# Soft experts on one Trainium2 core: the residual enters by VectorE and is turned back by the products that transpose the result

## The chip, the core and the metric

The kernel runs on one core of a Trainium2 chip. Five engines work side by side: TensorE (PE, with its weight loads listed as PEld), VectorE (DVE), ScalarE (ACT), GpSimd (POOL) and SyncE (SP, which here only issues DMAs). They are ordered by semaphores alone. The metric is the time of one execution in microseconds on the device. Lower is better.

## The reference

A small language-model tower: byte features, a neighbourhood attention, a mixture of experts of which two are used for each token, a decayed attention, and last a layer of soft experts. Every layer but the first adds its result to its input `h` after a layer norm. The last layer is the one that the change is about:

```python
def _L1_ffn_ref(x, Wr, br, W1, b1, g1, be1, m1, v1, W2, b2, g2, be2, m2, v2, Wo, bo):
    feat = jnp.mean(x, axis=0)
    w = jax.nn.softmax(feat @ Wr + br, axis=-1)
    h = jax.nn.relu(_bn(jnp.einsum('bfd,edh->bfeh', x, W1) + b1, g1, be1, m1, v1))
    h = jax.nn.relu(_bn(jnp.einsum('bfeh,ehk->bfek', h, W2) + b2, g2, be2, m2, v2))
    y = jnp.einsum('bfeh,ehd->bfed', h, Wo) + bo
    return jnp.einsum('bfed,fe->bfd', y, w)
...
h = h + _L1_ffn_ref(_layernorm(h, axis=-1), ...)
```

There are 32 batches (b) of 512 tokens (f) with 64 channels (d), and 8 experts (e), all in float32.

## The kernel before

**Layout.** Two batches make a pair; a pair is a tile of 128 partitions (64 channels of each batch) by 512 tokens. The residual stream `s.h` holds all 16 pairs in SBUF, and so does the normed input `s.z`, whose rows from 16 on are scratch (rows 16 to 19 hold the routing weights `f1_w` and row 20 the shift `f1_r` in the last layer).

**The turned basis.** Between the first layer and the last, `h` is kept multiplied by a 64x64 reflection (`house`, block-diagonal for the pair; `reflect` is its vector), which puts the mean of the channels into channel 0, so that the layer norm has no subtraction. A reflection is its own inverse. So the weights that write into `h` are turned once at the start: `turn_rows` (L600) takes blocks of 64 columns of `s.w_out` in four VectorE instructions (product with the vector L606, sum L609, outer product L612, subtraction L615). It runs inside `token_features`: steps 0 and 1 in the loop's round q = 5, step 2 in q = 6, step 3 in q = 7 (L860 to L867). TensorE waits for step 3 (L767) before the product L768 that turns the weights which read `h`; behind L768 on TensorE stand the last pair's tokens (L743), whose squares (GpSimd, L494) feed the last variance (L501), the norm's deviations (ACT, L798, L800) and then, by two DMAs, the first input of the next stage. Of the 18 blocks in `s.w_out` the first 9 are turned (`W_TURNED`); the last layer's output weights `f1_wo` and `raw_bo` are not among them.

**The last layer, `soft_experts` (L1816).** 64 steps, four for a pair, each for two experts (`ep`). A step has on TensorE `first` (4 products into `p_1`, L1853), `second` (4 into `p_2`, L1863) and `third` (2 into `p_y`, L1874, which sums over the pair's four steps); on ACT a ReLU between first and second (L1899, two instructions); on VectorE `weigh` between second and third (L1921: clamp and routing weight). TensorE issues them staggered and in this order in each round n: first of step n+3, second of n+2, third of n+1, turn of n. `second` waits for the ReLU of its own step and for `weigh` of the step before, as there is one `p_2`.

Once for each pair three more things happen. Ahead of the pair's first `third`, TensorE multiplies `house` with the pair's `h` into `p_y` (L1872), which brings the residual back to the plain basis. After its last `third`, VectorE adds the shift: `res = p_y + f1_r` (L1931), and TensorE turns `res` into rows of tokens by four 128x128 transposes with the identity (L1885, the stationary operand is every fourth column of `res`). ACT copies them (L1908) and SP writes them out (L1948). `third` of a new pair waits for `res` of the pair before. GpSimd does nothing in this stage.

**The stage ahead, `soft_router` (L1720),** computes the routing weights and the shift. Its L1765 is a full float32 product of 128x128 by 128x128, 16 times. The stages are separated by a barrier of all engines.

In the records each float32 product is two matmul instructions with a weight load each, and each float32 transpose is one.

Of the kernel before, what the change touches and what calls it, by code (L numbers as in the profile page):

```python
# [25 lines left out]
ALU = mybir.AluOpType  # L26
# [3 lines left out]
NB, T, D = 32, 512, 64  # L30
NP = NB // 2
NQ = NB // 4
# [3 lines left out]
EP = NE // 2  # L36
NH, DH = 8, 8
HL = NH // 2
ROUTES = 32
W_OUT, W_TURNED = 18, 9  # L40
KW, DIL = 31, 2
TG = T // DIL
QT = 32
# [82 lines left out]
def allocate(nc, ctx):  # L126
    s = Buffers()

    def sb(name, shape, dt=F32):
        return ctx.enter_context(nc.sbuf_tensor(name, shape, dt))  # L130

    s.const = sb("const", [128, CONST_COLS])
    s.h = sb("h", [128, NP, T])
    s.z = sb("z", [128, NB, T])
    s.pick = sb("pick_r", [128, EP, 128], F32R)
    s.winmask = sb("winmask_b", [128, 4, HL, WIN], BF16)
    s.ident_b = sb("ident_b", [128, 128], BF16)

    s.w1s = sb("tok_w1s", [128, HID])
    s.phase = sb("tok_phase", [128, 2, NQ])  # L140
    s.gram = sb("tok_gram", [128, 128])
    s.cross = sb("tok_cross", [128, NQ])
    s.bias_t = sb("tok_bias_t", [128, HID])
    s.tok_w2 = sb("tok_w2", [128, D])

    s.w_in = sb("w_in", [128, T])
    s.a0_wqk = s.w_in[:, 0:256].rearrange("p (c n) -> p c n", c=2)
    s.a0_wv, s.moe_wr, s.f1_wr, s.a1_wqk = s.w_in[:, 256:384], s.w_in[:, 384:416], s.w_in[:, 416:448], s.w_in[:, 448:512]
    s.moe_w1 = sb("moe_w1", [128, NE, D])
    s.f1_w1 = sb("f1_w1", [128, NE, D])  # L150
    s.w_out = sb("w_out", [128, W_OUT, D])
    s.a0_wp, s.moe_w2, s.f1_wo, s.raw_bo, s.raw_moe_b2, s.a1_wvk = [s.w_out[:, n:n + m, :] for n, m in ((0, 2), (2, EP), (10, EP), (14, EP), (6, 2), (8, 2))]
    s.moe_b2 = sb("moe_b2", [128, 128], F32R)
    s.a1_bvk = sb("a1_bvk", [128, 2, D])
    s.f1_br = sb("f1_br", [128, NE])
    s.f1_w2 = sb("f1_w2", [128, NE, D])
    s.f1_wdup = sb("f1_wdup", [128, EP, 2, D])
    s.f1_w = s.z[:, NP:NP + EP, :]
    s.f1_r = s.z[:, NP + EP, :]
    s.bn_diag = sb("bn_diag", [128, EP, 128])  # L160

    s.raw = sb("raw", [128, 3 * (NE + EP)])
    at = 0

    def part(*shape):
        nonlocal at
        n = int(np.prod(shape))
        at += n
        return s.raw[:, at - n:at]

    s.bn_var, s.bn_scale, s.bn_shift = part(NE + EP), part(NE + EP), part(NE + EP)
    s.loaded = ctx.enter_context(nc.semaphore("loaded"))
    s.bn_ready = ctx.enter_context(nc.semaphore("bn_ready"))
    s.sq, s.bc = [[sb(f"n_{x}{k}", [128, T]) for k in range(n)] for x, n in (("sq", 8), ("bc", 4))]
    s.rstd = sb("n_rstd", [128, NP // 4, T])
    s.n_sq, s.n_var, s.n_ln, s.n_rstd, s.n_z, s.n_zero, *s.n_hop = [ctx.enter_context(nc.semaphore("n_s_" + x)) for x in (
        "sq", "var", "ln", "rstd", "z", "zero", "hop0", "hop1", "hop2", "hop3")]
    s.n_bc = [ctx.enter_context(nc.semaphore(f"n_s_bc{k}")) for k in range(4)]
    s.spread = nc.dram_tensor("n_spread", (4, NP // 4, 128, T), F32).ap()
    s.eps = sb("eps", [128, 1])  # L180
    s.one = sb("one", [128, 1])

    s.cols = sb("cols", [128, COL_COUNT])
    return s
# [13 lines left out]
def const(s, name, rows=128):  # L198
    at, n = CONST_AT[name]
    return s.const[0:rows, at:at + n]  # L200
# [334 lines left out]
def done(n):  # L535

    return n + (1 + CREDITS)
# [7 lines left out]
def row(t, n):  # L545

    return t[:, bass.ds(n, 1), :].rearrange("p a b -> p (a b)")
# [70 lines left out]
def token_features(nc, s, a, windows):  # L618


    with ExitStack() as ctx:
# [12 lines left out]
        g = [s.z[:, 4 + 2 * n:6 + 2 * n, :] for n in range(4)]  # L634
        bias_rows = s.z[:, 12:14, :].rearrange("p a (q h) -> p (a q) h", h=HID)
        rstd = s.z[:, 14, :]
        tmp = s.z[:, NP + NQ:NP + NQ + 2, :].rearrange("p a (n d) -> p (a n) d", d=D)[:, 0:W_TURNED, :]
        split, own = sb("split", [64, T], 1, F32R)[0], sb("own", [64, NB, NF], 1, F32R)[0]
        squared, offset = sb("squared", [128, HID], 1)[0], sb("offset", [128, 1], 1)[0]
        total = sb("total", [128, W_TURNED + 2], 1)[0]  # L640
# [4 lines left out]
        block = ctx.enter_context(nc.Block())  # L645
# [1170 lines left out]
def soft_experts(nc, s, out):  # L1816


    with ExitStack() as ctx:
# [3 lines left out]
        def ps(name, shape, n=1):  # L1823
# [3 lines left out]
        a1, a2 = sb("a1", [128, 2, T]), sb("a2", [128, 2, T])  # L1827
        res, rows = sb("res", [128, T]), sb("rows", [128, 2, 4, D])
        p_1, p_2, p_y, p_t = ps("p1", [128, 2, T], 2), ps("p2", [128, 2, T])[0], ps("py", [128, T])[0], ps("pt", [128, T])[0]
        s_w1, s_a1, s_w2, s_a2, s_wo, s_res, s_t, s_rows, *s_zin = [  # L1830
            ctx.enter_context(nc.semaphore("se_" + x)) for x in ("w1", "s_a1", "w2", "s_a2", "wo", "s_res", "t", "s_rows", "zin0", "zin1")]
        s_out = [ctx.enter_context(nc.semaphore(f"se_out{k}")) for k in range(2)]
        block = ctx.enter_context(nc.Block())

# [2 lines left out]
            return at.k // EP, at.k % EP  # L1837

        half = [slice(0, 64), slice(64, 128)]

        @block.tensor
        def _(te):
            give_credits(te, s_w1, s_w2, s_wo, s_t)

            def first(at):
                slot, ep = where(at)
                if ep == 0:
                    te.wait_ge(s_zin[slot], at.of(8) * 32 + 32)
                te.wait_ge(s_a1, done(at.n - 2))
                for e2 in range(2):  # L1850
                    for b in range(2):
                        z = row(s.z, at.of(4)) if b == e2 else swapped[slot]
                        mm = nc.tensor.matmul(p_1[at.k % 2][half[b], e2, :], s.f1_w1[half[e2], 2 * ep + e2, :], z[half[e2], :],  # L1853
                                              start=True, stop=True, skip_group_check=True)
                mm.then_inc(s_w1, 1)

            def second(at):
                _, ep = where(at)
                te.wait_ge(s_a1, done(at.n))
                te.wait_ge(s_a2, done(at.n - 1))  # L1860
                for b in range(2):
                    for e2 in range(2):
                        mm = nc.tensor.matmul(p_2[half[e2], b, :], s.f1_w2[half[b], 2 * ep + e2, :], a1[at.k % 2][half[b], e2, :],  # L1863
                                              start=True, stop=True, skip_group_check=True)
                mm.then_inc(s_w2, 1)

            def third(at):
                _, ep = where(at)
                te.wait_ge(s_a2, done(at.n))
                if ep == 0:  # L1870
                    te.wait_ge(s_res, done(at.of(4) - 1))
                    nc.tensor.matmul(p_y[:], const(s, "house"), row(s.h, at.of(4)), start=True, stop=False, skip_group_check=True)  # L1872
                for b in range(2):
                    mm = nc.tensor.matmul(p_y[half[b], :], s.f1_wo[:, ep, :], a2[at.k % 2][:, b, :], start=False, stop=(ep == EP - 1),  # L1874
                                          skip_group_check=True)
                mm.then_inc(s_wo, 1)

            def turn(at):
                slot, ep = where(at)
                if ep == EP - 1:  # L1880
                    i = at.of(4)
                    te.wait_ge(s_res, done(i))
                    te.wait_ge(s_rows, done(i - 1))
                    for c in range(4):
                        mm = nc.tensor.transpose(p_t[:, c * 128:c * 128 + 128], res[slot][:, c::4], const(s, "ident"))  # L1885
                    mm.then_inc(s_t, 1)

            unrolled(EP * NP, 8, (3, first), (2, second), (1, third), (0, turn))
# [24 lines left out]
        @block.vector  # L1913
        def _(ve):
            give_credits(ve, s_a2, s_res)

            def weigh(at):
                _, ep = where(at)
                ve.wait_ge(s_w2, done(at.n))
                ve.wait_ge(s_wo, done(at.n - 2))  # L1920
                nc.vector.scalar_tensor_tensor(out=a2[at.k % 2][:], in0=p_2[:], scalar=col(s, "f1_be2", ep),  # L1921
                                               in1=s.f1_w[:, ep, :].unsqueeze(1).broadcast_to([128, 2, T]),
                                               op0=ALU.max, op1=ALU.mult).then_inc(s_a2, 1)

            def residual(at):
                slot, ep = where(at)
                if ep == EP - 1:
                    i = at.of(4)
                    ve.wait_ge(s_wo, done(at.n))
                    ve.wait_ge(s_t, done(i - 2))  # L1930
                    nc.vector.tensor_tensor(res[slot][:], p_y[:], s.f1_r, ALU.add).then_inc(s_res, 1)  # L1931

            unrolled(EP * NP, 8, (1, weigh), (0, residual))

# [56 lines left out]
```

## Time and profile before

| | |
|---|---|
| median of 3 runs | 989.21 us (987.61 to 993.39) |
| the profiled execution | 995.81 us, its span 993.8 us |
| granted TensorE clock, mean over the span | 0.932 of full speed |
| busy: PE, DVE, ACT, POOL | 87%, 53%, 47%, 27% |
| `soft_experts` | from 769 us to the end |

The span runs from the first to the last instruction of one execution; 2.0 us lie around it. Busy shares are means over the whole span. In the timeline rows below, a row is a run of instructions of one kind on one engine: its start, its length, and in brackets the engine's idle time before it with what ended that. Matmuls are pipelined: the length of one is longer than the distance from its start to the next one's start, so costs are taken from the distances.

### The profile page before, as it was taken

What the parts mean: (1) busy time and instruction counts of PE and PEld (TensorE: products, weight loads), DVE (VectorE), ACT (ScalarE), POOL (GpSimd) and SP (SyncE); (2) the same over time, 40 slices, a digit from 0 to 9 for tenths busy, and PEclk for the clock granted to TensorE, in tenths of its full rate; (3) what the DMA queues carried; (4) which work ended last, traced back from release to release, by engine and by line L of the source; (5) the groups of instructions that cost most, each with busy time, mean ns of one, the idle gap of its engine ahead of it and who ended that gap; (6) DMA issues with size and microseconds to landing.
All of it is one profiled execution on the core that took longest, in us unless ns stands there. A gap on an engine that the chain in (4) does not pass through costs nothing. (4 is left out here: it accounts for less than half of the span.)

```text
span 993.8 us, 28180 instructions
## 1 busy us (share of the span) xinstructions
PE 865.4 (87%) x12432; PEld 412.2 (41%) x12432; DVE 527.3 (53%) x719; ACT 469.4 (47%) x579; POOL 268.3 (27%) x270
## 2 busy tenths in 40 slices
PE   4796899989899994699999792988876899999997
PEld 2231577767667672122222120766644222222222
DVE  5443567757667673676675251656631344344443
ACT  3243477767777763344444442233321454444543
POOL 4044553524435233122211046324541000000000
PEclk9898899999999998799999796889977899999999
DMA  4201200010010011000000113223221111111110
GB/s 87 32 11 63 78 25 25 5 56 4 4 57 4 17 44 54 1 1 1 1 1 1 63 53 112 49 58 90 69 66 40 32 43 43 44 43 43 36 30 33
DMA packets 39771, 37.76 MB, mean 38 GB/s; under 512 B 21025, under 2 KB 25282, under 8 KB 39650
## 3 DMA queue, kind: packets, MB, share of 16 engines
q1 hardware_dynamic: 38578, 34.35, 12.6%
q8 instruction: 99, 1.62, 0.7%
q10 hardware_dynamic: 1072, 1.60, 0.5%
q14 instruction: 22, 0.18, 0.1%
HBM read 19.95 MB, written 7.60 MB: 28 GB/s over the span
## 5 line engine op out<-in xcount | busy, mean ns | idle before, releaser
L1921 DVE SCALAR_TENSOR_TENSOR se_a<-se_p,cols,z 128x1024 f32<-128x1024 f32 x64 | 82.1, 1284 | 137.9 <-PE se_p L1863 137.9
L1899 ACT ACTIVATE se_a<-se_p,cols 128x512 f32<-128x512 f32 x128 | 92.6, 773 | 81.9 <-PE se_p L1853 81.9
L1189 DVE TENSOR_REDUCE na_rowmax<-na_ps 128x16 f32<-128x1024 f32 x64 | 78.0, 1218 | 77.6 <-PE na_ps L1065 77.6
L1481 DVE TENSOR_TENSOR me_gw<-me_pc,me_g 128x1024 f32<-128x1024 f32 x64 | 78.3, 1223 | 76.3 <-PE me_pc L1336 71.7
L1377 ACT ACTIVATE me_g<-me_p,cols 128x1024 f32<-128x1024 f32 x64 | 71.3, 1114 | 86.7 <-PE me_p L1324 82.0
L923 POOL TENSOR_TENSOR z<-na_k,const 128x512 f32<-128x512 f32 x64 | 64.5, 1039 | 141.2 <-ACT na_k L1129 141.2
L494 POOL TENSOR_TENSOR n_sq<-h 128x512 f32<-128x512 f32 x64 | 67.4, 1058 | 110.8 <-DVE h L846 43.8
L529 POOL TENSOR_TENSOR z<-h,n_bc 128x512 f32<-128x512 f32 x62 | 78.5, 1283 | 25.5 <-DMA n_bc<-n_spread 25.5
L1324 PE MATMUL me_p<-z,moe_w 64*64 64x512 f32 x512 | 74.0, 650 | 6.4 <-ACT me_g L1377 6.4
L1192 DVE TENSOR_TENSOR na_e<-na_ps,na_rowmax 128x1024 f32<-128x1024 f32 x64 | 78.3, 1224 | 2.2
L1853 PE MATMUL se_p<-z,f_w 64*64 64x512 f32 x256 | 71.2, 628 | 4.0 <-DMA se_zswap<-z 4.0
L1074 PE MATMUL na_pt<-const,na_e 128*128 128x128 f32 x512 | 69.2, 278 | 2.5 <-ACT na_et L1159 1.7
L1346 PE MATMUL me_py<-me_gw,w_out 128*64 128x512 f32 x256 | 70.8, 632 | 0.4 <-DVE me_gw L1481 0.4
L1853 PE MATMUL se_p<-se_zswap,f_w 64*64 64x512 f32 x256 | 70.3, 628 | 0.0
L1874 PE MATMUL se_py<-se_a,w_out 128*64 128x512 f32 x256 | 69.0, 618 | 0.4 <-DVE se_a L1921 0.4
L1159 ACT ACTIVATE na_et<-na_pt 128x1024 f32<-128x1024 f32 x64 | 65.4, 1022 | 7.8 <-PE na_pt L1074 7.0
L1863 PE MATMUL se_p<-se_a,f_w 64*64 64x512 f32 x512 | 67.4, 597 | 1.1 <-DVE se_a L1921 1.1
L1152 ACT ACTIVATE na_e<-na_e 128x1024 f32<-128x1024 f32 x64 | 67.4, 1053 | 1.7 <-DVE na_e L1192 1.3
L1263 POOL TENSOR_TENSOR h<-h,me_added 128x512 f32<-128x512 f32 x16 | 20.6, 1290 | 155.3 <-DVE me_added L1489 155.3
L1074 PEld LDWEIGHTS na_pt<-const,na_e 128*128 128x128 f32 x512 | 56.0, 140 | 13.9 <-issue 11.2
L1146 ACT ACTIVATE na_v<-na_pm 64x512 f32<-64x512 f32 x64 | 38.6, 602 | 33.7 <-PE na_pm L1025 33.3
L1091 PE MATMUL na_po<-na_v,na_et 128*32 128x18 f32 x4096 | 49.4, 187 | 4.1 <-issue 2.7
(282 smaller groups left out, 1274.9 us busy)
## 6 DMA issues: line engine op xcount, KB each, us to landing
n_bc<-n_spread SPq DMA_DIRECT2D x128, 128.0 KB, 3.0
da_zswap<-z SPq DMA_DIRECT2D x32, 128.0 KB, 2.4
se_zswap<-z SPq DMA_DIRECT2D x32, 128.0 KB, 2.3
out<-se_rows SPq DMA_DIRECT2D x16, 256.0 KB, 2.1
n_spread<-n_rstd SPq DMA_DIRECT2D x13, 256.0 KB, 2.0
const<-in_const ACTq DMA_DIRECT2D x1, 712.0 KB, 6.5
const<-in_const ACTq DMA_DIRECT2D x1, 562.0 KB, 4.2
f_w<-in_L_ffn_W SPq DMA_DIRECT2D x4, 128.0 KB
```

The source lines that it names most:

```text
L529: return eng.tensor_tensor(row(s.z, p), row(s.h, p), s.bc[p % 4][:], ALU.mult)
L1074: mm = nc.tensor.transpose(p_t[:, c, :], e[b][:, 2 * c:2 * c + 2, :].rearrange("p h w -> p (h w)"), const(s, "ident"))
L1189: nc.vector.tensor_reduce(rowmax[b][:], scored, AX, ALU.max).then_inc(s_max, 1)
L1192: nc.vector.tensor_tensor(e[b][:], scored, rowmax[b][:].unsqueeze(2).broadcast_to([128, GROUPS, WIN]), ALU.subtract).then_inc(s_diff, 1)
L1324: mm = nc.tensor.matmul(p_1[half[e2], b, :], s.moe_w1[half[b], 2 * ep + e2, :], row(s.z, at.of(4))[half[b], :], start=True, stop=True, ski ...
L1346: mm = nc.tensor.matmul(p_y[slot][half[b], :], s.moe_w2[:, ep, :], gw[at.k % 2][:, b, :], start=False, stop=(ep == EP - 1), skip_group_che ...
L1377: nc.scalar.activation(g[at.k % 2][:], p_1[:], ACT.Gelu, bias=col(s, "moe_b1", ep)).then_inc(s_g, 1)
L1481: nc.vector.tensor_tensor(gw[at.k % 2][:], p_c[:], g[at.k % 2][:], ALU.mult).then_inc(s_gw, 1)
L1853: mm = nc.tensor.matmul(p_1[at.k % 2][half[b], e2, :], s.f1_w1[half[e2], 2 * ep + e2, :], z[half[e2], :], start=True, stop=True, skip_grou ...
L1874: mm = nc.tensor.matmul(p_y[half[b], :], s.f1_wo[:, ep, :], a2[at.k % 2][:, b, :], start=False, stop=(ep == EP - 1), skip_group_check=True)
L1899: ins = nc.scalar.activation(a1[at.k % 2][:, e2, :], p_1[at.k % 2][:, e2, :], ACT.Relu, scale=col(s, "f1_g1", 2 * ep + e2), bias=col(s, "f ...
L1921: nc.vector.scalar_tensor_tensor(out=a2[at.k % 2][:], in0=p_2[:], scalar=col(s, "f1_be2", ep), in1=s.f1_w[:, ep, :].unsqueeze(1).broadcast ...
```

## The change

In `soft_experts` the product of `house` with `h` is taken out. The first `third` of a pair starts the sum in `p_y` itself. GpSimd adds the shift to `h` of all 16 pairs at the start of the stage; VectorE adds `h` (now with the shift in it) instead of the shift. The result is then still in the turned basis, and the four transposes become four float32 products with `house` in place of the identity, which transpose and turn back at once. So that `f1_wo` and `raw_bo` write into the turned basis, the blocks of `s.w_out` are put in another order, and the first 17 of 18 are turned.

```diff
-W_OUT, W_TURNED = 18, 9
+W_OUT, W_TURNED = 18, 17
...
-    s.a0_wp, s.moe_w2, s.f1_wo, s.raw_bo, s.raw_moe_b2, s.a1_wvk = [s.w_out[:, n:n + m, :] for n, m in ((0, 2), (2, EP), (10, EP), (14, EP), (6, 2), (8, 2))]
+    s.f1_wo, s.raw_bo, s.a0_wp, s.moe_w2, s.raw_moe_b2, s.a1_wvk = [s.w_out[:, n:n + m, :] for n, m in ((0, EP), (4, EP), (8, 2), (10, EP), (14, 2), (16, 2))]
...
-        tmp = s.z[:, NP + NQ:NP + NQ + 2, :].rearrange("p a (n d) -> p (a n) d", d=D)[:, 0:W_TURNED, :]
+        tmp = s.z[:, NP + NQ:NP + NQ + 3, :].rearrange("p a (n d) -> p (a n) d", d=D)[:, 0:W_TURNED, :]
...
+        @block.gpsimd
+        def _(pool):
+            for p in range(NP):
+                nc.gpsimd.tensor_tensor(row(s.h, p), row(s.h, p), s.f1_r, ALU.add).then_inc(s_shifted, 1)
...
                 if ep == 0:
                     te.wait_ge(s_res, done(at.of(4) - 1))
-                    nc.tensor.matmul(p_y[:], const(s, "house"), row(s.h, at.of(4)), start=True, stop=False, skip_group_check=True)
                 for b in range(2):
-                    mm = nc.tensor.matmul(p_y[half[b], :], s.f1_wo[:, ep, :], a2[at.k % 2][:, b, :], start=False, stop=(ep == EP - 1),
+                    mm = nc.tensor.matmul(p_y[half[b], :], s.f1_wo[:, ep, :], a2[at.k % 2][:, b, :], start=(ep == 0), stop=(ep == EP - 1),
                                           skip_group_check=True)
...
-                        mm = nc.tensor.transpose(p_t[:, c * 128:c * 128 + 128], res[slot][:, c::4], const(s, "ident"))
+                        mm = nc.tensor.matmul(p_t[:, c * 128:c * 128 + 128], res[slot][:, c::4], const(s, "house"), start=True, stop=True, skip_group_check=True)
...
                     ve.wait_ge(s_wo, done(at.n))
+                    ve.wait_ge(s_shifted, i + 1)
                     ve.wait_ge(s_t, done(i - 2))
-                    nc.vector.tensor_tensor(res[slot][:], p_y[:], s.f1_r, ALU.add).then_inc(s_res, 1)
+                    nc.vector.tensor_tensor(res[slot][:], p_y[:], row(s.h, i), ALU.add).then_inc(s_res, 1)
```

## Rows read from the trace of the kernel before

**Rows 1.** The page: span, and the granted TensorE clock in 40 slices.
```profile
span 993.8 us, 28180 instructions
...
PEclk9898899999999998799999796889977899999999
```

**Rows 2.** The page: the chain that ended last, by line, share of the span.
```profile
PE se_p L1853 7%; PE se_py L1874 6%; PE se_p L1863 6%; PE se_py L1872 2%; PE se_pt L1885 1%; DVE se_a L1921 0%; DMA se_zswap<-z 0%; DVE se_res L1931 0%; ACT se_rows L1908 0%; SPq L1944 0%; PEldq L542 0%
```

**Rows 3.** Busy time by stretch: PE, PEld, DVE, ACT, POOL, clock, DMA, GB/s.
```profile
768.00:784.00 16.00, 11.34 (x63) 2.75 (x62) 2.57 (x2) 5.65 (x9) 0.00 (x0) 0.79 0.14 33
784.00:988.00 204.00, 203.12 (x1314) 57.48 (x1310) 88.53 (x77) 96.46 (x137) 0.00 (x0) 1.00 0.14 38
```

**Rows 4.** Timeline, one pair of `soft_experts`, from its `house` product to the next.
```profile
859.07 1.12 PE L1872 MATMUL se_py<-h,const 128*128 128x512 f32 x2
...
860.13 1.08 PE L1874 MATMUL se_py<-se_a,w_out 128*64 128x512 f32 x4
...
861.14 0.75 PE L1885 MATMUL se_pt<-const,se_res 128*128 128x128 f32 x4
...
861.82 0.64 PE L1853 MATMUL se_p<-z,f_w 64*64 64x512 f32 x1
...
869.61 1.28 DVE L1921 SCALAR_TENSOR_TENSOR se_a<-se_p,cols,z 128x1024 f32<-128x1024 f32 x1 [1.60 <-PE se_p L1863]
...
870.81 0.68 DVE L1931 TENSOR_TENSOR se_res<-se_py,z 128x512 f32<-128x512 f32 x1
...
871.39 1.04 PE L1863 MATMUL se_p<-se_a,f_w 64*64 64x512 f32 x8
...
872.35 1.12 PE L1872 MATMUL se_py<-h,const 128*128 128x512 f32 x2
```

**Rows 5.** Timeline, `soft_router`: full products L1765 (16) and L1769 (4), ACT's copies.
```profile
758.26 6.39 PE L1765 MATMUL sr_p<-const,sr_wide 128*128 128x128 f32 x32 [2.98 <-DVE sr_wide L1813]
...
762.08 0.60 ACT L1781 ACTIVATE z<-sr_p 128x512 f32<-128x512 f32 x1 [1.11 <-PE sr_p L1765]
763.78 0.60 ACT L1781 ACTIVATE z<-sr_p 128x512 f32<-128x512 f32 x1 [1.11 <-PE sr_p L1765]
...
764.49 3.60 PE L1769 MATMUL sr_p<-z,f_wdup 128*128 128x512 f32 x8
...
764.69 0.60 ACT L1781 ACTIVATE z<-sr_p 128x512 f32<-128x512 f32 x1 [0.31 <-PE sr_p L1765]
```

**Rows 6.** Busy time by stretch, the last of these products (columns as in rows 3).
```profile
763.80:764.70 0.90, 0.90 (x9) 0.88 (x8) 0.00 (x0) 0.59 (x2) 0.00 (x0) 1.00 0.00 0
```

**Rows 7.** Weight loads of two transposes by line: ns least/median/most, L1885 and L1037.
```profile
L1885 PEld LDWEIGHTS se_pt<-const,se_res x64: 195/209/219, 794.7 to 989.5; 128*128 128x128 f32 x64
```
```profile
L1037 PEld LDWEIGHTS na_pm<-const,z x64: 138/142/144, 135.3 to 381.8; 128*128 128x128 f32 x64
```

**Rows 8.** Timeline, end of `token_features`: the turning of `w_out` and what follows.
```profile
72.53 1.36 DVE L606 TENSOR_TENSOR z<-w_out,const 128x576 f32<-128x576 f32 x1
...
73.92 0.76 DVE L609 TENSOR_REDUCE tf_total<-z 128x9 f32<-128x576 f32 x1
...
75.63 1.61 DVE L846 TENSOR_SCALAR h<-tf_pm,cols 128x512 f32<-128x512 f32 x2 [0.95 <-PE tf_pm L743]
...
81.63 0.96 DVE L615 TENSOR_TENSOR w_out<-w_out,z 128x576 f32<-128x576 f32 x1
...
82.85 1.13 PE L768 MATMUL tf_pz<-w_in,const 128*128 128x512 f32 x2
```

**Rows 9.** The same turning of a single block of 64 columns, lines L606 and L615.
```profile
L606 DVE TENSOR_TENSOR z<-tok_w,const x1: 216/216/216, 35.7 to 35.7; 128x64 f32<-128x64 f32 x1
```
```profile
L615 DVE TENSOR_TENSOR tok_w<-tok_w,z x1: 226/226/226, 36.5 to 36.5; 128x64 f32<-128x64 f32 x1
```

**Rows 10.** GpSimd's two-input instructions of 128x512 by line: ns least/median/most.
```profile
L494 POOL TENSOR_TENSOR n_sq<-h x64: 1032/1039/1554, 52.7 to 735.6; 128x512 f32<-128x512 f32 x64
```
```profile
L529 POOL TENSOR_TENSOR z<-h,n_bc x62: 1258/1276/1442, 95.4 to 749.7; 128x512 f32<-128x512 f32 x62
```

More of the change, by code:

```diff
@@ L1829, in soft_experts @@
         p_1, p_2, p_y, p_t = ps("p1", [128, 2, T], 2), ps("p2", [128, 2, T])[0], ps("py", [128, T])[0], ps("pt", [128, T])[0]
-        s_w1, s_a1, s_w2, s_a2, s_wo, s_res, s_t, s_rows, *s_zin = [
-            ctx.enter_context(nc.semaphore("se_" + x)) for x in ("w1", "s_a1", "w2", "s_a2", "wo", "s_res", "t", "s_rows", "zin0", "zin1")]
+        s_w1, s_a1, s_w2, s_a2, s_wo, s_shifted, s_res, s_t, s_rows, *s_zin = [
+            ctx.enter_context(nc.semaphore("se_" + x)) for x in ("w1", "s_a1", "w2", "s_a2", "wo", "shifted", "s_res", "t", "s_rows", "zin0", "zin1")]
         s_out = [ctx.enter_context(nc.semaphore(f"se_out{k}")) for k in range(2)]
```

## The prediction

> **What bounds the kernel now.** I read the page first, for the span and the clock [rows 1], then the chain that ended last [rows 2]. The chain's longest parts are `first`, `third` and `second` of the last layer, with the `house` product (L1872) at 2% and the transposes (L1885) at 1% of the span: this stage's end is TensorE's. The share of busy time over the whole span would not say that much, so I asked for the stage alone. From 784 to 988 us TensorE is busy 203.1 of 204.0 us, at a granted clock of 1.00, while VectorE has 88.5, ScalarE 96.5 and GpSimd nothing [rows 3]. So in this stage one microsecond of TensorE's stream taken out is one microsecond of the kernel, as long as no other engine comes up behind it. Last I looked at one pair instruction by instruction [rows 4], since each pair has the same pattern.
>
> **What leaves: the `house` product.** It starts at 859.07 and the next group starts at 860.13, so it holds TensorE for 1.06 us [rows 4]. There is one for each of 16 pairs: 16 x 1.06 = 17.0 us. All of it lies on the path.
>
> **What comes in its place: four products for four transposes.** The transposes hold TensorE from 861.14 to 861.82, 0.68 us [rows 4]. This stage has no full product of 128x128 by 128x128, but the stage ahead has 16 of them in a row. ScalarE copies each four as they end: from 762.08 to 763.78 is 1.70 us for four at the slow clock, from 763.78 to 764.69 is 0.91 us for four [rows 5], and the stretch of these last four shows the clock at 1.00 [rows 6]. So inside a row of them a product costs 0.23 us at full clock, 0.114 us for each of its two instructions. Two things are different in the change. First, a group pays for its edges. In a row of eight instructions of 512 columns (L1769, 3.60 us with 0.59 for the last) one follows the other by 0.43 us [rows 5]; the two of `house` would be 0.86, and take 1.06, so the edges cost 0.20 us. Second, the stationary operand here is every fourth column of `res`, and the weight loads of such transposes take 209 ns against 142 ns for the adjacent columns of the attention stage [rows 7]; how much of that is hidden under a product no row shows. From the rows: lower end, loads wholly hidden and half of the edges too, 0.91 + 0.10 = 1.01 us; upper end, one strided load takes its place in the row. Four strided transposes with four such loads take 0.68 with their edges; less 0.20 for the edges this is 0.12 a load, so eight loads are 0.96, with edges 1.16, and I go to 1.20. I take 1.13, nearer the upper end because its operand is the same one. The turn becomes 1.13 - 0.68 = 0.45 us longer for each pair (0.33 to 0.52): 16 x 0.45 = 7.2 us. The last pair's turn, after which only a copy and the store come, is one of the 16.
>
> Net of the two: 16 x (-1.06 + 0.45) = -9.8 us (-11.7 to -8.6).
>
> **Does TensorE stay the bound?** `second` waits for `weigh` of the step before. `weigh` started at 869.61 and ended at 870.89, and the next `second` starts at 871.39: 0.50 us of slack in a step that has neither `house` nor a turn in it [rows 4]. With `house` gone every step looks like this one or has the longer turn in addition, so this slack is not cut. The other wait is that of the pair's first `third` for `res`: `res` ends at 871.49, and TensorE comes to that place at 872.35, where `house` stood behind the same wait [rows 4]. 0.86 us of slack, the same as before. The turn comes 1.06 us earlier behind it and waits for the same `res`; it is then at 873.4. None of this turns into a wait.
>
> **GpSimd's 16 additions.** Two inputs of 128x512 in float32: such instructions take 1.04 us (squares) or 1.28 us (the norm's product) [rows 10]. 16 of them are 17 to 20 us, from about 769 on, so done by 790. GpSimd has nothing else in the stage [rows 3], and no DMA is queued behind it. VectorE's new wait is for one addition per pair; the first `res` comes only after four steps of 2.9 us behind the filling at 781, so the wait is met by 10 us, and behind it on VectorE stands the next `weigh`. That VectorE's instruction now reads `h` and not the shift costs nothing: same shapes, both in SBUF. What can cost is GpSimd and VectorE at SBUF together. While the pipeline fills, TensorE does wait for `weigh` (1.28 us [rows 4]), twice. In the running steps the 0.50 us slack covers it. If `weigh` is slower by the ratio 1.28 to 1.04 that GpSimd's own two kinds show, it is 0.30 us each, 0.6 us; at best nothing. I take 0.2 us.
>
> **Turning 17 blocks and not 9.** Four VectorE instructions grow from 576 to 1088 columns. L606 took 216 ns for 64 columns and 1357 for 576: 2.23 ns a column; L615 226 and 959: 1.43 ns a column [rows 8, 9]. For 512 columns more: step 0 +1.14, steps 2 and 3 +0.73 each, the sum (0.76 us for 576) at most +0.68. Steps 0 and 1 have 0.95 us of idle behind them [rows 8]; 1.82 us more makes the next tokens 0.87 us late, and those lie under ScalarE's work for the last quads, with three banks to go round. Step 2 likewise falls into a wait for TensorE. Step 3 is not covered: it ended at 82.59, and TensorE stood ready for L768 at 82.85 [rows 8]. It will end at 81.63 + 1.69 = 83.32, TensorE starts L768 at about 83.45, 0.6 us late. The last pair's tokens, its square, the last variance, the deviations and the DMAs of the next stage stand behind that, all in one chain, so the whole 0.6 us is paid. Bounds: 0.2 (some of it is absorbed) to 1.5 us (step 3 grows as step 0 did and steps 0 and 1 are not wholly covered). Moving the blocks in `s.w_out` changes addresses, no sizes: nothing.
>
> **Sum.** -9.8 + 0.2 + 0.6 = -9.0 us. Against the profiled execution: 995.81 - 9.0 = 986.8, span 984.8. That execution was 6.6 us above the median of the three runs, 989.21; most of this work is the same in every run, so the median becomes 980.2 us. With the bounds: -11.7 + 0 + 0.2 = -11.5 and -8.6 + 0.6 + 1.5 = -6.5, so 977.7 to 982.7.
>
> **The rivals.**
>
> (a) Loads are not hidden. The turn is then eight strided loads of 0.209 us [rows 7], 1.67, with edges about 1.87 us: +1.19 against 0.68. Per pair +0.13, in all +2.1, with the other terms +2.9: 992.1 us, slower than before. If load and stream strictly take turns (0.209 + 0.107, a quarter of the 0.43 for 512 columns), it is 2.53 us, +0.79 per pair, +13.4 in all, 1002.6. It decides from a turn of 1.74 us, that is 0.22 us for each instruction. Against it: four such loads with their transposes went by in 0.68 us, 0.17 each with the edges [rows 4], and full products in a row took 0.114 [rows 5], so loads of adjacent columns are hidden. For it: no row has a strided load between float32 products. 6%.
> The Trainium skill, TensorE: Matmul & The Clock Gate, in The mechanism of its part on packing small matmuls, says that a weight load overlaps running matmuls "only when row_grp differs". All eight instructions use the whole array, so by that rule (a) would hold and the sum would be positive. The row of full products speaks against it, since 0.91 us for four leaves no room for eight loads beside the stream.
>
> (b) Something else takes TensorE's place, so that only part comes back: `weigh` with GpSimd beside it, or ScalarE, whose copy of the turned rows now waits for a longer turn. If half of the 9.8 us is lost it is 985.1 us. Against it: VectorE is busy 43% and ScalarE 47% of the stretch [rows 3], and the additions last only 20 us of 220. 5%.
>
> (c) The clock. It changed level many times between 390 and 777 us [rows 1] while stages with gaps ran. A shift of 0.6 us ahead of them can move such a change. The three runs of one kernel already lie 5.8 us apart, which I put down to this. It adds 2 us to either side of the range and is no case of its own sign; that the median of the kernel before is itself taken from three runs is in it too. Inside the last layer the clock stays at 1.00, as TensorE has no more gaps than it had.
>
> (d) The change does not do what it says, the compiler keeping the product or the transposes as they were: no sign of it, since each is an instruction of its own line. 1%.
>
> **How the numbers follow.** My forecast, 977.7 to 982.7 by its own bounds, has 88%. With 2 us for the clock and the medians it is 975.7 to 984.7. Rivals (b) and (a) lie outside and hold 11%, so the range needs little more than the forecast's own: 975.5 to 985.2. A measurement of this kernel can tell about 0.5% (4.9 us) from no change, so faster is below 984.3, slower above 994.2. Faster: 0.88 of the forecast, less its upper edge with the clock against it, plus a part of (b): 0.87. Slower: the strict form of (a) and mishaps of the clock: 0.04. Same: 0.09.
>
> **What would show it right or wrong.** In the profile after: no row of L1872; one pair from `first` to `first` in 13.28 - 0.61 = 12.67 us; the turn at 1.0 to 1.2 us from its first product to the next `first`, 64 products as 128 instructions; `second` and `third` without idle time ahead of them after 784; GpSimd's additions over by 790; `weigh` still at 1.28 us, or up to 1.6 in the first 20 us. L615 at about 1.69 us, and L768 0.6 us later than 82.85. If the turn takes 1.7 us or more, (a) was right; if VectorE or ScalarE appears in the chain after 784, (b) was.

## The result: slower by 0.6 per cent

The median of nine runs is 998.52 us (995.76 to 999.43), against 992.24 us (986.94 to 995.49) for nine runs of the kernel before. The ratio is 1.0059, with a 95% interval of 1.0037 to 1.0081. The profiled execution took 998.22 us, its span is 996.3 us (before [rows 1]).

The page of the changed kernel, its chain by line (before [rows 2]). The lines have moved: `first` is L1858, `second` L1868, `third` L1878, the turn L1889, `weigh` L1925, the addition L1936, the copy L1912.

```profile
PE se_p L1858 7%; PE se_py L1878 6%; PE se_p L1868 6%; PE se_pt L1889 3%; DVE se_a L1925 0%; DMA se_zswap<-z 0%; DVE se_res L1936 0%; ACT se_rows L1912 0%; SPq L1949 0%; PEldq L542 0%
```

The 2% of the `house` product are gone, and the turn (the four products that transpose `res`) has gone from 1% to 3% of the span. So the chain is still TensorE's; what was taken out came back in the turn. The busy time of the last stage, in the columns of [rows 3]:

```profile
781.00:991.00 210.00, 208.33 (x1341) 74.52 (x1341) 88.27 (x78) 95.85 (x135) 4.72 (x4) 1.00 0.13 36
```

TensorE is as full as before (208.3 of 210 us) at a clock of 1.00, VectorE and ScalarE are no nearer to being the bound. What has grown is the time of weight loads: 74.5 us in 210, against 57.5 in 204.

One turn in the timeline, with the next `first` behind it, and then two turns in the chain in order of time (start, length):

```profile
803.15 2.13 PE L1889 MATMUL se_pt<-const,se_res 128*128 128x128 f32 x8
805.21 0.64 PE L1858 MATMUL se_p<-z,f_w 64*64 64x512 f32 x1
```
```profile
803.22 2.06 PE se_pt L1889 x8
...
816.83 2.06 PE se_pt L1889 x8
```

The turn holds TensorE from 803.15 to 805.21, 2.06 us, where the transposes took 0.68 [rows 4]. A pair takes 816.83 - 803.22 = 13.61 us; it was 13.28. So each pair lost 1.38 us and won 1.06, and 16 pairs give 16 x 0.33 = 5.3 us of the 6.3 between the medians. The weight loads of that line (least, median, most, in ns):

```profile
L1889 PEld LDWEIGHTS se_pt<-const,se_res x128: 308/329/332, 789.5 to 991.6; 128*128 128x128 f32 x128
```

329 ns for a load, where the transposes' load of the same columns of the same tile had 209 [rows 7]. That is the first sight of the cause. The length of a load's record is not its price, though: in the transposes the records last 209 ns and the instructions follow each other by 0.12 us. Prices are taken from the distances between starts, as before.

### The profile page after: what moved, and what is told of

Same layout as the page of the kernel before. It is cut to its first block and busy times, and to the rows that moved or that the text cites. A ratio compares the mean times of both kernels' runs of the same rounds, so it can differ in the third digit from the quotient of the medians.

```text
span 996.3 us, 28260 instructions
## 1 busy us (share of the span) xinstructions
PE 867.4 (87%) x12464; PEld 429.2 (43%) x12464; DVE 529.7 (53%) x719; ACT 470.0 (47%) x579; POOL 289.3 (29%) x286
## 5 line engine op out<-in xcount | busy, mean ns | idle before, releaser
L1925 DVE SCALAR_TENSOR_TENSOR se_a<-se_p,cols,z 128x1024 f32<-128x1024 f32 x64 | 82.2, 1284 | 141.5 <-PE se_p L1868 141.5
L1324 PE MATMUL me_p<-z,moe_w 64*64 64x512 f32 x512 | 71.5, 629 | 6.4 <-ACT me_g L1377 6.4
L1858 PE MATMUL se_p<-z,f_w 64*64 64x512 f32 x256 | 71.1, 628 | 4.0 <-DMA se_zswap<-z 4.0
L1858 PE MATMUL se_p<-se_zswap,f_w 64*64 64x512 f32 x256 | 70.3, 628 | 0.0
L1878 PE MATMUL se_py<-se_a,w_out 128*64 128x512 f32 x256 | 69.0, 618 | 0.4 <-DVE se_a L1925 0.4
L1868 PE MATMUL se_p<-se_a,f_w 64*64 64x512 f32 x512 | 67.3, 596 | 1.1 <-DVE se_a L1925 1.1
```

What stands on the lines that cost most here:

```text
L1324: mm = nc.tensor.matmul(p_1[half[e2], b, :], s.moe_w1[half[b], 2 * ep + e2, :], row(s.z, at.of(4))[half[b], :], start=True, stop=True, ski ...
```

## The experiments

Two theories stood after the result. **S:** the load of every fourth column of a float32 tile, ahead of a product, takes about 0.23 us, longer than the stream of 128 columns, and sets the pace. The stream is estimated at 0.107 us, a quarter of the 0.43 for 512 columns [rows 5]. **R:** in this place a weight load for the whole array isn't hidden at all under a float32 product, so load (0.12 us) and stream (0.107 us) follow each other, which also makes 0.23 us. A turn of eight instructions has some 0.20 us of edges, so an instruction costs (turn - 0.20) / 8: here 0.233 us.

### Adjacent columns

```diff
-nc.tensor.matmul(p_t[:, c * 128:c * 128 + 128], res[slot][:, c::4], const(s, "house"), ...)
+nc.tensor.matmul(p_t[:, c * 128:c * 128 + 128], res[slot][:, c * 128:c * 128 + 128], const(s, "house"), ...)
...
-nc.vector.tensor_tensor(res[slot][:], p_y[:], row(s.h, i), ALU.add)
+nc.vector.tensor_tensor(res[slot][:].rearrange("p (c t) -> p c t", c=4), p_y[:].rearrange("p (t c) -> p c t", c=4),
+                        row(s.h, i).rearrange("p (t c) -> p c t", c=4), ALU.add)
```

> The changed kernel, but VectorE writes `res` so that the 128 columns of each of the four products lie next to each other; the products then load adjacent columns. Same result. Theory S (a float32 load of every fourth column takes about 0.23 us and sets the pace): the turn falls from 2.06 us to 8 x 0.112 + 0.2 = 1.09, a pair from 13.61 to 12.64 us, in all 16 x 0.97 = 15.5 us less than the changed kernel and about 9.5 us less than the kernel before (ratio 0.990). Rival R (a weight load for the whole array is not hidden under a float32 product in this place, whatever its columns): the turn stays at about 2.06 us and the ratio at 1.006. Whether VectorE pays for reading p_y in the new order: 0.68 us if not; it has 0.86 us of slack.

Measured: 981.89 us median of 4 runs, ratio to the kernel before 0.9897 (0.9858 to 0.9936); the kernel before had 990.47 beside it. The chain, two turns in a row:

```profile
840.26 1.09 PE se_pt L1889 x8
...
852.89 1.09 PE se_pt L1889 x8
```
```profile
L1889 PEld LDWEIGHTS se_pt<-const,se_res x128: 186/192/192, 789.6 to 976.6; 128*128 128x128 f32 x128
L1936 DVE TENSOR_TENSOR se_res<-se_py,h x16: 1048/1086/1094, 787.1 to 974.7; 128x512 f32<-128x512 f32 x16
```

The turn is 1.09 us, (1.09 - 0.20) / 8 = 0.111 us for an instruction, and a pair is 12.63 us, as S had it. R is out as it stands: on TensorE nothing but the distance of the columns was changed, and 0.111 us for an instruction leaves no room for a load behind a stream of 0.107. That only the load of distant columns stays unhidden is still possible; the long stream below decides it. VectorE does pay: its addition takes 1.09 us in place of 0.68. That lies in slack.

### The change with transposes in place of the products

```diff
-nc.tensor.matmul(p_t[:, c * 128:c * 128 + 128], res[slot][:, c::4], const(s, "house"), start=True, stop=True, ...)
+nc.tensor.transpose(p_t[:, c * 128:c * 128 + 128], res[slot][:, c::4], const(s, "ident"))
```

> The changed kernel with the four transposes by the identity, as before; the turning back is left out, so the output stays in the turned basis. It does the rest of the change alone: no `house` product, GpSimd's additions, 17 blocks turned. Both theories: the turn is 0.68 us, a pair 12.22 us, so 16 x 1.06 = 17.0 us less in the last layer; the turning of 17 blocks gives back 0.5 to 0.6 us; about 16.4 us less than before (ratio 0.983). If it is much less, a term other than the products was wrong.

Measured: 973.3 us median of 4 runs, ratio 0.9819 (0.9783 to 0.9855), that is 17.2 us under the 990.47 of the kernel before. In the timeline:

```profile
847.83 0.75 PE L1889 MATMUL se_pt<-const,se_res 128*128 128x128 f32 x4
...
860.06 0.75 PE L1889 MATMUL se_pt<-const,se_res 128*128 128x128 f32 x4
```

A pair takes 860.06 - 847.83 = 12.23 us, so all the rest of the change is worth 13.28 - 12.23 = 1.05 us for a pair, the whole `house` product. The other terms of the sum, -16.2 us together, stood within the spread of the runs (ratio 0.9819 is -17.9, its interval -21.5 to -14.4): the loss lies in the four products. It also shows that the same columns of the same tile, in the same place, load fast enough for a transpose.

### Is the load slow, or is it not hidden?

```diff
-nc.tensor.matmul(p_t[:, c * 128:c * 128 + 128], res[slot][:, c::4], const(s, "house"), ...)
+nc.tensor.matmul(p_t[:], res[slot][:, c::4], const(s, "cos"), ...)
```

> The changed kernel, each of the four products with a moving operand of 512 columns (the cosine table) in place of 128 columns of `house`; the output is meaningless. The loads are the same eight strided ones, the stream beside each is four times as long (0.43 us). If a strided load takes about 0.23 us by itself and runs beside the stream, it is hidden: the turn is 8 x 0.43 + 0.2 to 0.3 = 3.6 to 3.7 us, a pair 15.2. If load and stream take turns (0.12 + 0.107 made the 0.233 us): 8 x 0.55 = 4.4 and an edge, 4.5 us, a pair 16.1.

Measured: 1024.34 us in a single run; what is read from it is the turn, at a granted clock of 1.00.

```profile
788.86 3.75 PE se_pt L1889 x8
...
804.16 3.75 PE se_pt L1889 x8
```

The turn is 3.75 us and a pair 15.30. Eight streams of 0.43 us are 3.44; only 0.31 is left for the edges and the first load. If each of the seven loads behind the first added 0.12 us, it would be 4.5 us. So the slow load runs beside the stream and disappears under it when the stream is long enough. In the changed kernel the stream is about 0.107 us and the load is the longer of the two. The Trainium skill, TensorE: Matmul & The Clock Gate, in its section The mechanism, says that weight loads overlap running products only when the row group differs. Here and with adjacent columns all instructions use the whole array, and the loads are hidden (3.75 and 1.09 us a turn), so the runs do not bear that rule out.

### The load's time by the distance of its columns

```diff
-... res[slot][:, c::4] ...
+... res[slot][:, c // 2 * 256 + c % 2:c // 2 * 256 + 256:2] ...
...
+nc.vector.tensor_tensor(res[slot][:].rearrange("p (a t b) -> p a t b", a=2, b=2), p_y[:].rearrange("p (t a b) -> p a t b", a=2, b=2),
+                        row(s.h, i).rearrange("p (t a b) -> p a t b", a=2, b=2), ALU.add)
```

> The changed kernel, with `res` written so that each product loads every second column. Same result. Every fourth column gave 0.233 us for an instruction, adjacent ones 0.112, the stream alone 0.107. If the load's time grows with the distance of the columns, it is at most about 0.17 us here, and a turn between 1.09 and 1.55; if any distance over one costs the whole price, it is 0.233 and 2.06 us; if the price begins beyond two, 1.09 us.

```diff
-... res[slot][:, c::4] ...
+... res[slot][:, c:c + 382:3] ...
```

> The changed kernel, each product loading every third column of `res`; the output is meaningless. Together with every second and every fourth it gives the load's time by distance: growing in proportion 0.175 to 0.20 us for an instruction, the turn 1.5 to 1.8 us; with one price for all distances 0.233 and 2.06 us.

A turn of every second column, and then one of every third:

```profile
813.57 1.14 PE se_pt L1889 x8
```
```profile
819.98 1.59 PE se_pt L1889 x8
```
```profile
L1889 PEld LDWEIGHTS se_pt<-const,se_res x128: 194/197/197, 788.1 to 975.5; 128*128 128x128 f32 x128
```
```profile
L1889 PEld LDWEIGHTS se_pt<-const,se_res x128: 251/261/263, 793.6 to 988.2; 128*128 128x128 f32 x128
```

The starts of the single instructions in the traces, without any term for the edges, give the same to 0.001 us.

| distance of the columns | turn, us | an instruction, us | median load, ns |
|---|---|---|---|
| 1 | 1.09 | 0.111 | 192 |
| 2 | 1.14 | 0.118 | 197 |
| 3 | 1.59 | 0.174 | 261 |
| 4 | 2.06 | 0.233 | 329 |

From 2 to 4 the time of an instruction is 0.058 us times the distance (0.117, 0.175, 0.233). At 1 the instruction takes little more than the stream's 0.107 us, so the load's own price there is not seen. From two on the load goes as if it paid for each element that it passes over, and a distance of two is nearly free. The two kernels ran once each, 981.66 and 994.46 us; the verdict rests on the turns, which agree within 0.003 us over all pairs of a run, not on these times.

### The transposes of before, adjacent

The same reordering of `res` in the kernel before, with its transposes and its `house` product.

> The kernel before, with `res` written so that the four transposes load adjacent columns. Same result. The attention stage's transposes of adjacent columns load in 142 ns where these take 209. Theory S: the turn falls from 0.68 to about 0.55 us, 16 x 0.13 = 2 us less (ratio 0.998). Rival R: nothing changes.

Measured: 990.51 us median of 10 runs, ratio 0.9995 (0.9968 to 1.0022), so the time can't tell. In the profile, the loads and one turn with the next `first`:

```profile
L1885 PEld LDWEIGHTS se_pt<-const,se_res x64: 138/140/143, 797.7 to 991.3; 128*128 128x128 f32 x64
```
```profile
876.80 0.66 PE L1885 MATMUL se_pt<-const,se_res 128*128 128x128 f32 x4
877.38 0.64 PE L1853 MATMUL se_p<-z,f_w 64*64 64x512 f32 x1
```

The load goes from 209 to 140 ns, and a turn from 0.68 to 0.59 us by the starts of its instructions, 1.4 us in all 16. The expectation had 0.55. From start to start a transpose behind the first takes 0.109 us here and 0.120 in the kernel before. Distance does cost a transpose something, but a small part of what it costs a product.

### The turning of 17 blocks alone

The changed kernel's order of the blocks and `W_TURNED = 17`, with the last layer of the kernel before.

> The kernel before with only the turning of 17 blocks and their new order; the last layer is as before, so it multiplies with output weights in the turned basis and its result is not the reference's. By the prediction's step the whole costs 0.6 us and no more than 1.5 (ratio 1.0006, not to be told from 1). In the profile: L615 near 1.49 us in place of 0.96, the product behind it (L768) about 0.4 us later against the tokens ahead of it. By what the profile of the changed kernel shows, the first product of the next stage comes only 0.2 us later than before.

Measured: 993.89 us median of 10 runs, ratio 1.0004 (0.9966 to 1.0042). The timeline of this kernel, from the last scaling ahead of the turning:

```profile
72.88 0.68 DVE L841 TENSOR_TENSOR z<-tf_pm,z 128x512 f32<-128x512 f32 x1
...
82.58 1.49 DVE L615 TENSOR_TENSOR w_out<-w_out,z 128x1088 f32<-128x1088 f32 x1
```
```profile
84.12 1.12 PE L768 MATMUL tf_pz<-w_in,const 128*128 128x512 f32 x2 [0.26 <-DVE w_out L615]
...
97.63 2.08 PE L992 MATMUL na_pm<-z,w_in 128*128 128x512 f32 x2 [7.28 <-POOL z L529]
```

And the kernel before, in the same view:

```profile
71.93 0.68 DVE L841 TENSOR_TENSOR z<-tf_pm,z 128x512 f32<-128x512 f32 x1
...
96.71 1.22 PE L992 MATMUL na_pm<-z,w_in 128*128 128x512 f32 x1 [7.64 <-POOL z L529]
```

From that scaling L768 is 84.12 - 72.88 = 11.24 us away; in the kernel before it was 82.85 - 71.93 = 10.92 (L768 in [rows 8]). So the step costs TensorE 0.32 us here, and the next stage's first product (L992) is 24.75 us away, where it was 24.78. What was lost is not seen any more behind the two DMAs that lie between. The last stage's first product came at 774.8 us in this profile, against 772.1 before and 769.1 with the whole change: the stages between differ by that much from one profile to another, more than this edit.

### The reordering by scattered writes

The products load adjacent columns, as in the first experiment; the addition reads in order and writes with jumps of 128 elements.

```diff
+nc.vector.tensor_tensor(res[slot][:].rearrange("p (c t) -> p t c", c=4), p_y[:].rearrange("p (t c) -> p t c", c=4),
+                        row(s.h, i).rearrange("p (t c) -> p t c", c=4), ALU.add)
```

> The adjacent columns of before again (same result), but VectorE reads p_y and h in order and writes `res` scattered, where the other order read every fourth element and took 1.09 us in place of 0.68. If reading apart is what costs, 0.68 us here; if either does, 1.09. The addition has 0.86 us of slack in a pair, so the time moves only by the last pair: ratio 0.990 either way. Theory S has a turn of 1.09 us again.

Measured: 982.62 us median of 10 runs, ratio 0.992 (0.9894 to 0.9946), with 991.99 us for the kernel before beside it.

```profile
813.56 1.09 PE se_pt L1889 x8
```
```profile
L1936 DVE TENSOR_TENSOR se_res<-se_py,h x16: 1033/1054/1065, 785.7 to 973.3; 128x512 f32<-128x512 f32 x16
```

The same turn, and VectorE pays either way, 1.05 us here. With every second column it paid nothing, 0.68 us:

```profile
L1936 DVE TENSOR_TENSOR se_res<-se_py,h x16: 679/680/692, 785.6 to 973.9; 128x512 f32<-128x512 f32 x16
```

## Why the prediction was wrong

It forecast 980.2 us and a gain with a chance of 0.87; the kernel became slower. The step that failed is **"What comes in its place"**, its 1.13 us for the turn. It measured 2.06.

- **The price of a strided load.** I worked out 0.12 us a load from the four strided transposes, called that the upper end, and said that no row shows how much of a strided load is hidden under a product. The number was right for a transpose and nothing followed from it for a product: the same columns ahead of a product take 0.233 us. The upper end of 1.20 us was therefore no bound. With the measured 2.06 in the sum, 16 x (-1.06 + 1.38) = +5.1 us, and with the other terms +5.9, where the medians of nine runs differ by 6.3. This term alone is 16 x 0.93 = 14.9 of the 18.3 us between forecast and measurement.
- **The starting point.** Another 3.0 us are the median of the kernel before: 989.21 us from three runs, 992.24 from nine. The forecast allowed 2 us for this and for the clock together.
- **The row of full products** [rows 5] gave 0.114 us, and adjacent columns in the last layer gave 0.111. So that reading was right, but it was a reading of adjacent columns. The two sources, strided transposes and adjacent products, each lacked one half of the case, and I took the case to lie between them. It lay outside both.
- **Rival (a)** had the direction, loads that set the pace, and the turn of 1.74 us from which it decides; it gave 1.87 us and 992.1 us, and stood at 6%. That its 0.209 us came near the measured 0.233 is luck. It is the length of a transpose's load record, and those transposes followed each other by 0.12 us. In the products too the records are longer than the pace: 192 ns at 0.111 us, 197 at 0.118, 261 at 0.174, 329 at 0.233. Read as a pace, 192 ns would have made the turn of adjacent columns 1.74 us, where it took 1.09. Its heading, that loads are not hidden, and its strict form, load and stream in turns, are what the long stream excludes. Its chance was too low: with no row for the operand it should have stood near the forecast, and the range, up to 985.2, should have held it.
- **The `house` product**, 1.06 us each: right, 1.05 in the run that keeps the transposes.
- **TensorE stays the bound**: right. In the changed kernel TensorE was busy 208.3 of 210 us, and with the addition at 1.09 us 189.8 of 191.1, with no wait for VectorE before the last pair.
- **GpSimd's additions**: they ran from 766.0 to 785.7 us at 1.28 us each, and `weigh` beside them took 1.28 us as before, so 0 and not 0.2 us.

```profile
766.03 19.69 POOL L1844 TENSOR_TENSOR h<-h,z 128x512 f32<-128x512 f32 x16 [18.72 <-POOLq L1723]
```
```profile
774.53 1.28 DVE L1925 SCALAR_TENSOR_TENSOR se_a<-se_p,cols,z 128x1024 f32<-128x1024 f32 x1 [19.16 <-PE se_p L1868]
```

- **The turning of 17 blocks**: forecast 0.6 us. Step 3 grew to 1.49 us, not 1.69: between 576 and 1088 columns it costs 1.04 ns a column, and I had taken the slope of 1.43 from a single block of 64 up. TensorE lost 0.32 us and the stage behind it nothing that shows. Inside the bounds, or a little under them.
- **The clock**: the last stage began 3.0 us earlier than in the profile of before, though nothing ahead of it got faster, which is why the spans differ by only 2.5 us and the stage by 5.5. Chance, not the change, is enough for that: the eight profiles of kernels with the same code ahead of this stage begin it between 767.0 us (the transposes) and 774.8 us (the turning alone), which is more than the 2 us to either side that I had allowed. The start goes roughly with the mean clock granted from 390 to 767 us, 0.89 and 0.87 in these two; what moved the clock was not tested.

```profile
390.00:767.00 377.00, 306.55 (x2324) 133.08 (x2325) 200.38 (x338) 135.74 (x152) 117.01 (x103) 0.89 0.15 44
```
```profile
390.00:767.00 377.00, 310.69 (x2321) 133.63 (x2322) 199.56 (x338) 135.66 (x151) 115.04 (x101) 0.87 0.15 43
```

What stays open is why a float32 product's load of distant columns takes twice the transpose's. In the records a product has two instructions with a load each, a transpose one, but the two loads of one product are equally long, so the count alone does not explain 0.233 against 0.12 for each. With adjacent columns too the product's load has the longer record, 192 ns against 140, though the pace is nearly the same, 0.111 and 0.109 us. Only float32 tiles were tried, so whether elements or bytes make the distance is not known either.

The version that the experiments point to keeps the whole change and stores `res` in the order in which the products read it: 981.89 us, ratio 0.9897, faster than both. With it the forecast's sum would have held: -9.0 us forecast, 0.9897 is -10.2 us (the interval -14.1 to -6.3), and 0.992 with the scattered writes is -7.9.

## What to carry to other kernels

A float32 weight load has a price of its own that depends on how far apart its columns lie, and it shows only when the stream beside it is shorter: compare the two for the very operand and the very kind of instruction. Take the price from the distance between starts, not from the length of the load's record. When a transpose is replaced by a product, the transpose's load is not a bound for the product's. If the producer can write the operand in the order in which TensorE loads it, on an engine with slack, that is the whole cure; here even every second column would do, at no cost to VectorE.

## What the runs showed of the hardware

- A float32 load of 128 columns ahead of a product takes 0.233 us at a distance of four elements, 0.174 at three, 0.118 or less at two, and at one it is hidden, at 0.111 us for load and stream together. A transpose's instruction goes from 0.109 to 0.12 us between distance one and four.
- The Trainium skill, TensorE: Matmul & The Clock Gate, section LDWEIGHTS, reckons a load by its number of columns alone; an estimate by its formula is 107 ns for 128 columns. The pace at distances one and two, 0.111 and 0.118 us, does not contradict that; at three and four the measurement decides, and it is 1.6 and 2.2 times as much.
- A load for the whole array is hidden under a product of the whole array: 0.43 us of stream covered a 0.23 us load.
- VectorE's float32 addition of 128x512 with one input in PSUM takes 0.68 us in order, 1.09 us when it reads every fourth element, 1.05 us when it writes with jumps of 128, and 0.68 us when pairs of elements stay together.
